# Narrow tiles of a mixture-of-experts tail: gathers ahead of the stores, half buffers for the results, low parts made ahead of the results

## The chip, the core and the metric

One core of a Trainium2 chip runs the whole program. The metric is the device time of one execution in microseconds (us). The kernel before took 1560.92 us (median of three runs, 1560.53 to 1563.27). TensorE (PE) multiplies, VectorE (DVE) and ScalarE (ACT) move and transform what it leaves in PSUM, GpSimd (POOL) issues the indirect DMAs here, SyncE (SP) the plain ones.

## The reference, cut to what matters

The program is a gated cross-attention layer over 16 batches of 256 tokens, followed by a mixture of experts on the normalised rows:

```
x = x + tanh(g_xattn) * cross_attention(ctx, layernorm(x))     # 8 heads of 128
gates = (layernorm(x) @ Wg + bg) / (1 + 1e-6)                  # 8 experts
w, idx = top_k(gates, 2); w = softmax(w)
h = silu(layernorm(x) @ W1[e] + b1[e])                         # 256 -> 1024
y[e] = h @ W2[e] + b2[e]                                       # 1024 -> 256
x = x + tanh(g_ffn) * sum over the two chosen e of w[e] * y[e]
```

All products are made as three passes over a high and a low part of both sides (`product`, L181 to L183: high times low, low times high, high times high). Only the end of the experts' part is touched by the change.

## The kernel before

The 4096 tokens, each with two experts, make 8192 pairs, which are sorted by expert into lists padded to rows of 128 pairs (71 such rows). A tile is the work on one or two of these rows for one expert. The first 31 tiles (`WIDE`) are wide, two rows each; the last 9 (tiles 31 to 39, `NARROW`) are narrow, one row each, since an expert's list can end in half a wide tile. A wide tile takes four steps n on TensorE, a narrow one two; step 124 (`FIRST_N`) is the first narrow one and step 141 the last.

For each tile: POOL gathers the tile's token rows into `xg` (`gather`); TensorE turns them into `px` (`turn_x`); ScalarE and VectorE split them into `xt_hi` and `xt_lo`. For each step TensorE makes the hidden part `ph` (`hidden`) from `xt` and the split first-layer weights `w1s_hi` and `w1s_lo`. In narrow tiles VectorE copies this part to `flat` (`read_flat`), and TensorE turns it with the identity (`turn_hidden`, L1293; the target is called `ph` or `routing`). ScalarE applies silu (`hs`) and makes `ht_hi`, VectorE makes `ht_lo` (`lo_h`, L1664), and TensorE multiplies with the second-layer weights into `py` (`out`). After a tile's last step VectorE's `finish` adds the bias into `yo` (L1700) and multiplies by the pair's weight (L1706). POOL then stores the rows, adding them to the output in memory (`scatter`, L901). SyncE loads 1 MB of first-layer weights per tile (L716) when the low parts of the tile two before are made.

The order on each engine is the order in which the code is written; nothing schedules it. TensorE's loop over n does `turn_x` (every second narrow step), `hidden(n)`, `turn_hidden(n-1)`, `out(n-2)`. So between two `out` pieces stand a hidden part and a turn. VectorE's loop over n does `read_flat(n)`, on even steps `lo_x` and `take_weights`, on odd steps `finish` of the tile before, then `lo_h(n-1)` and the low part of the weights of step n+2 (`w1_lo_two`, L1654). `finish(t)` waits until TensorE's last `out` of tile t is done, reads the expert's number into a register (L619), and waits until the buffer of `yo` is free.

Each added store waits for the one before it (`s_add`), because two of them may touch the same output row. There are two `yo` buffers of two rows; narrow tiles use only the first row of each. POOL's loop over t issues, in this order, the second store of tile t-2 (wide tiles only), the gathers of tile t+2 (or t+3 for narrow ones), the first store of tile t-1. For `xg` there are two buffers of two rows, of which narrow tiles use all four rows in turn.

Of the kernel before, what the change touches and what calls it, by code (L numbers as in the profile page):

```python
# [9 lines left out]
ALU = mybir.AluOpType  # L10
# [4 lines left out]
B, T, D = 16, 256, 256  # L15
# [23 lines left out]
WIDE = (ROWS - NARROW) // 2  # L39
assert 2 * WIDE + NARROW == ROWS and WIDE % 2  # L40
SUB = 2
TILE = SUB * P
N_TILES = WIDE + NARROW
# [41 lines left out]
def subs(t):  # L85
    return SUB if t < WIDE else 1


def row_of(t):
    return SUB * t if t < WIDE else SUB * WIDE + t - WIDE  # L90
# [6 lines left out]
def blocks_of(t):  # L97
    return PB if t < WIDE else 2 * PB


def step_of(t):
    return PARTS * t if t < WIDE else PARTS * WIDE + (t - WIDE) * (FT // (2 * PB))


N_STEPS = step_of(N_TILES)
TILE_OF = [(t, j) for t in range(N_TILES) for j in range(steps_of(t))]

N_RAW, N_PH, N_HS, N_HT, N_XT, N_XG, N_YO = 2, 3, 2, 3, 2, 2, 2
N_W1S = PARTS
LAG = 2  # L110
LEAD = 2
# [219 lines left out]
def layer(nc, programs, A, sem, alloc, space, early, step, work, lists, ident, iota8, lane, dram,  # L331
# [6 lines left out]
    with ExitStack() as ctx:  # L338
# [102 lines left out]
        with ExitStack() as banks:  # L441
            def bank(name):
                return banks.enter_context(nc.psum_tensor(name, [P, 512], F32))
# [11 lines left out]
        with ExitStack() as banks:  # L455
# [3 lines left out]
            py = [over[last_o], bank("py1")]  # L459
# [53 lines left out]
        N_GN = N_XG * SUB  # L513
# [9 lines left out]
        s_l2, s_pyr, s_w, s_yo, s_add = sem("y_pair"), sem("y_read"), sem("w_ready"), sem("y_out"), sem("added")  # L523
# [30 lines left out]
        def w1_parts(n):  # L554

            if n >= N_STEPS or TILE_OF[n][0] < EARLY and TILE_OF[n][0] != HOME_TILES[0]:
                return []
            t, j = TILE_OF[n]
            k = blocks_of(t) // PB
            return [(t, j * k + i) for i in range(k)]  # L560
# [13 lines left out]
        def xg_of(t, s):  # L574
            n = t - WIDE
            return xg[t % N_XG][s] if n < 0 else xg[t % N_XG][n // N_XG % SUB]

        def s_gathered(t):
            return s_g[t % N_XG] if t < WIDE else s_gn[(t - WIDE) % N_GN]

# [4 lines left out]
        def had_rows(t):  # L585

            n = t - WIDE
            return t - N_XG if n < N_XG else WIDE - N_XG + n % N_XG if n < N_GN else t - N_GN
# [26 lines left out]
        def home_of(t):  # L615
            return int(t >= HOME_TILES[0])
# [156 lines left out]
        def _(pool):  # L773
# [39 lines left out]
            def norm_rows(b):  # L813

                pool.wait_ge(s_mvc, b + 1)
                own.mark(pool.tensor_scalar(ve["c"][:, 0:TT], mv_c[:, 0:TT, 1], EPS, 1.0, ALU.add, ALU.mult))
                pow_rstd("c", rs_c, TT, s_rsc)
                negate(mv_c)
                own.wait()
                pool.wait_ge(s_rsc, b + 1)  # L820
                if b >= 2:
                    pool.wait_ge(s_rowst[b % 2], 16 * (b // 2))
                elif b == 0:
                    pool.wait_ge(s_pad, 16 * N_PAD)
                for t in range(TT):
                    last = norm(rows[b % 2][:, t, 0:D], x2[b % 2][:, t, :], mv_c, rs_c, t)
                last.then_inc(s_xn, 1)
# [16 lines left out]
            def list_tokens(b):  # L844

                pool.wait_ge(s_place, b + 1)
                pool.wait_ge(s_pad, 16 * N_PAD)
                if b >= EARLY_B:
                    pool.wait_ge(s_early_names, 32)
                for k in range(TOP):  # L850
                    for t in range(TT):
                        q = k * TT + t
                        pool.indirect_dma_start(
                            out=dram["lists"].rearrange("l (p o) -> (l p) o", o=1),
                            out_offset=bass.IndirectOffsetOnAxis(ap=place[:, q:q + 1].bitcast(U32), axis=0),
                            in_=ids[:, TT * b + t:TT * b + t + 1], in_offset=None,
                        ).then_inc(s_listed, 16)
# [22 lines left out]
            def gather(t, s):  # L880
                if t >= N_XG:

                    pool.wait_ge(s_px, had_rows(t) + 1)
                    pool.wait_ge(s_w, row_of(had_rows(t) + 1))
                u = row_of(t) + s
                source = dram["xhat"][0:EARLY_B * T, :] if t < EARLY else dram["xhat"]
                pool.indirect_dma_start(
                    out=xg_of(t, s)[:, :], out_offset=None, in_=source,
                    in_offset=bass.IndirectOffsetOnAxis(ap=token[:, u:u + 1].bitcast(U32), axis=0),
                ).then_inc(s_gathered(t), 16)  # L890

            def scatter(t, s):
                u = row_of(t) + s
                pool.wait_ge(s_yo, u + 1)
                if u:

                    pool.wait_ge(s_add, 16 * u)
                else:
                    for i in range(2):
                        pool.wait_ge(s_x2st[i], 16 * (B // 2))  # L900
                pool.indirect_dma_start(  # L901
                    out=A["out"], out_offset=bass.IndirectOffsetOnAxis(ap=token[:, u:u + 1].bitcast(U32), axis=0),
                    in_=yo[t % N_YO][:, s, :], in_offset=None, compute_op=ALU.add,
                ).then_inc(s_add, 16)

            for c in range(2):
# [28 lines left out]
                gather(2, s)  # L935
            norm_rows(B - 1)
            for t in range(1, N_TILES + 1):
                if t >= 2 and subs(t - 2) == 2:
                    scatter(t - 2, 1)
                if t + N_XG == EARLY:  # L940
                    pool.wait_ge(s_rowst[1], 16 * (B // 2))
                    pool.wait_ge(s_token, 1)
                for later in (t + N_XG, t + N_XG + 1):
                    if later < N_TILES and (later < WIDE + N_XG) == (later == t + N_XG):
                        for s in range(subs(later)):
                            gather(later, s)
                if t == 2:
                    pool.wait_ge(s_row, 1)
                    pool.wait_ge(s_listed, 16 * TOP * TT * B)
                    pool.indirect_dma_start(  # L950
                        out=names[0:LATE_SUB, 0:P], out_offset=None, in_=dram["lists"],
                        in_offset=bass.IndirectOffsetOnAxis(ap=row[0:LATE_SUB, :].bitcast(U32), axis=0),
                    ).then_inc(s_names, 16)
                scatter(t - 1, 0)
                if t == 1:
                    list_tokens(B - 1)
# [444 lines left out]
        def _(dve):  # L1401
# [249 lines left out]
            def w1_lo_two(t, part):  # L1651
                dve.wait_ge(s_w1hi, w1_before(t) + part + 2)
                hi, lo = (two_parts(s, part) for s in w1s)
                dve.tensor_tensor(lo, raw_parts(t, part), hi.bitcast(F32), ALU.subtract).then_inc(s_w1lo, 2)  # L1654
# [30 lines left out]
            def finish(t):  # L1685

                dve.wait_ge(s_l2, step_of(t + 1))
                if t < EARLY:
                    if t == 0:
                        dve.wait_ge(s_home_b2, 32)  # L1690
                    bias = home_b2[:, home_of(t), :]
                else:
                    e = expert_of(dve, t)
                    if t == EARLY:
                        dve.wait_ge(s_b2, 16)
                    bias = b2[:, bass.ds(e * D, D)]
                if t >= N_YO:
                    dve.wait_ge(s_add, 16 * row_of(t - N_YO + 1))
                n = subs(t)
                dve.tensor_tensor(yo[t % N_YO][:, 0:n, :], py[t % 2][:, 0:n * D].rearrange("p (s d) -> p s d", s=n),  # L1700
                                  bias.unsqueeze(1).to_broadcast([P, n, D]), ALU.add).then_inc(s_pyr, 1)
                dve.wait_ge(s_pyr, t + 1)
                for s in range(n):
                    u = row_of(t) + s
                    dve.wait_ge(s_w, u + 1)
                    dve.tensor_scalar(yo[t % N_YO][:, s, :], yo[t % N_YO][:, s, :], wcol[:, u:u + 1], None, ALU.mult)\  # L1706
                        .then_inc(s_yo, 1)

            def first_spread(half, scale, add):
# [106 lines left out]
            for n in range(2, FIRST_N):  # L1816
                t, j = TILE_OF[n]
# [26 lines left out]
            for n in range(FIRST_N, N_STEPS + 1):  # L1844
                if n < N_STEPS:
                    t, j = TILE_OF[n]
                    read_flat(n)
                    if j == 0 and t + 1 < N_TILES:
                        lo_x(t + 1)
                        take_weights(t + 1)  # L1850
                    if j == 1:
                        finish(t - 1)
                if n > FIRST_N:
                    lo_h(n - 1)
                for t, part in w1_parts(n + LEAD)[::2]:
                    w1_lo_two(t, part)
            finish(N_TILES - 1)


# [21 lines left out]
```

## Time and profile before

| | |
|---|---|
| median of three runs | 1560.92 us |
| the profiled execution's own time | 1558.27 us |
| its span, from the first to the last instruction | 1556.6 us |
| mean granted TensorE clock | 0.99 |
| narrow tiles: from the first narrow px to the last py | 1470.1 to 1546.8 us |

Times in the rows below are microseconds from the start of the span. A timeline row gives the start, the duration, engine, line, operation, what it writes and reads, and in brackets how long its engine sat idle before it and what ended this. The durations of matmuls overlap (they are pipelined), so an engine's pace is read from one start to the next. A row of busy time by stretch gives the stretch and its length, then busy us with the number of instructions for PE, PEld (weight loads), DVE, ACT and POOL, then the granted clock (1.00 is 2.4 GHz), the share of time in which DMA engines were busy, and GB/s.

### The profile page before, as it was taken

The page shows a single profiled execution, that of the slowest core. Times are in us where ns is not written, and L with a number is a line of the kernel's source. Part 1 is how long each engine was busy: PE and PEld are TensorE (multiplying, and loading weights), DVE is VectorE, ACT ScalarE, POOL GpSimd, SP SyncE. Part 2 cuts the span into 40 slices and gives each one's busy share as a digit, 9 for nine tenths or more (in the row PEclk, how much of TensorE's full clock was granted, in tenths as well). Part 3 has the DMA queues.
Part 4 walks back from the last instruction along what each step waited for, and adds up shares of the span by engine and source line. Part 5 has one row for each costly group of instructions (what it writes and reads, how often), then busy time and mean ns, then how long its engine had stood idle before and what let it go on. Part 6 is the DMA issues. An engine that isn't in the chain of part 4 may idle for free. (4 is left out here: it accounts for less than half of the span.)

```text
span 1556.6 us, 29904 instructions
## 1 busy us (share of the span) xinstructions
PE 1503.6 (97%) x10410; PEld 1386.2 (89%) x10410; DVE 1110.2 (71%) x2687; ACT 950.6 (61%) x2060; POOL 604.3 (39%) x714
## 2 busy tenths in 40 slices
PE   6999998999999999999999999999989999999986
PEld 5889887888989889898888988888989999999986
DVE  6777776777777777777777777777786666666674
ACT  5655654565565555555565565555777777777764
POOL 5322423233342433433234342332454544444452
PEclk9999999999999999999999999999999999999998
DMA  4000100001000000000000000022754544554553
GB/s 147 19 21 8 21 8 21 8 22 28 8 22 8 22 28 8 22 8 21 12 17 29 7 22 8 8 75 70 193 128 127 154 131 127 146 139 127 147 157 69
DMA packets 57823, 91.13 MB, mean 59 GB/s; under 512 B 8521, under 2 KB 44774, under 8 KB 57550
## 3 DMA queue, kind: packets, MB, share of 16 engines
q1 hardware_dynamic: 41710, 70.19, 14.0%
q0 software_dynamic: 15824, 18.98, 6.9%
q8 instruction: 88, 1.44, 0.4%
q14 instruction: 57, 0.47, 0.1%
q10 hardware_dynamic: 144, 0.05, 0.0%
HBM read 70.91 MB, written 18.29 MB: 57 GB/s over the span
## 5 line engine op out<-in xcount | busy, mean ns | idle before, releaser
L876 POOL TENSOR_SCALAR probs<-probs,rsum 128x512 f32<-128x512 f32 x256 | 174.1, 692 | 531.6 <-DVE rsum L1547 523.7
L1087 ACT ACTIVATE pt_hi<-turn 128x512 fp32r<-128x512 f32 x256 | 139.3, 595 | 239.7 <-PE turn L1233 239.7
L901 POOL DMA_INDIRECT out_rows<-yo,token x71 | 121.5, 1711 | 213.5 <-DMA out_rows<-yo,token 137.6
L1664 DVE TENSOR_TENSOR ht_lo<-hs,ht_hi 128x512 fp32r<-128x512 f32 x142 | 98.0, 690 | 114.5 <-ACT ht_hi L1052 113.0
L1541 DVE TENSOR_REDUCE smax<-score 128x1 f32<-128x512 f32 x256 | 169.8, 685 | 12.8 <-PE score L183 12.4
L986 ACT ACTIVATE probs<-score,nbias 128x512 f32<-128x512 f32 x256 | 173.0, 685 | 4.2 <-DVE nbias L1543 4.1
L1043 ACT ACTIVATE hs<-ph,vecs 128x256 f32<-128x256 f32 (+1 forms) x284 | 114.2, 457 | 95.6 <-PE ph L183 82.4
L1772 DVE TENSOR_TENSOR pt_lo<-turn,pt_hi 128x512 fp32r<-128x512 f32 x256 | 164.2, 682 | 9.4 <-ACT pt_hi L1087 9.3
L181 PE MATMUL py<-w_hi,ht_lo 128*128 (+1 forms) x568 | 163.9, 289 | 5.8 <-DVE ht_lo L1664 5.8
L182 PE MATMUL py<-w_lo,ht_hi 128*128 (+1 forms) x568 | 161.8, 285 | 0.0
L183 PE MATMUL py<-w_hi,ht_hi 128*128 (+1 forms) x568 | 161.7, 285 | 0.0
L181 PE MATMUL ring<-pt_hi,v_lo 128*128 128x256 f32 x512 | 146.9, 287 | 10.7 <-DVE kt_lo L1444 9.0
L974 ACT ACTIVATE kt_hi<-ring,vecs 128x512 fp32r<-128x512 f32 x128 | 88.3, 690 | 94.5 <-PE ring L183 94.5
L181 PE MATMUL ph<-xt_hi,w1s_lo 128*128 128x256 f32 x496 | 141.4, 285 | 4.7 <-DVE xt_lo L1642 4.6
L183 PE MATMUL ring<-pt_hi,v_hi 128*128 128x256 f32 x512 | 145.5, 284 | 0.0
L182 PE MATMUL ring<-pt_lo,v_hi 128*128 128x256 f32 x512 | 145.3, 284 | 0.0
L183 PE MATMUL ph<-xt_hi,w1s_hi 128*128 128x256 f32 x496 | 139.0, 280 | 0.0
L182 PE MATMUL ph<-xt_lo,w1s_hi 128*128 128x256 f32 x496 | 138.8, 280 | 0.0
L1444 DVE SCALAR_TENSOR_TENSOR qt_lo<-ring,vecs,qt_hi 128x256 fp32r<-128x256 f32 x128 | 61.9, 484 | 106.9 <-ACT qt_hi L976 105.4
L1233 PEld LDWEIGHTS turn<-ident,probs 128*128 128x128 f32 x1024 | 121.4, 142 | 17.4 <-POOL probs L876 0.3
L1233 PE MATMUL turn<-ident,probs 128*128 128x128 f32 x1024 | 134.3, 275 | 0.0
L1444 DVE SCALAR_TENSOR_TENSOR kt_lo<-ring,vecs,kt_hi 128x512 fp32r<-128x512 f32 x128 | 95.9, 749 | 50.7 <-ACT kt_hi L974 42.9
(247 smaller groups left out, 4709.7 us busy)
## 6 DMA issues: line engine op xcount, KB each, us to landing
w_raw<-in_L_ffn_W SPq DMA_DIRECT2D x45, 1024.0 KB, 12.8
xhat_rows<-rows SPq DMA_DIRECT2D x16, 264.0 KB, 2.2
x_raw<-in_x SPq DMA_DIRECT2D x16, 256.0 KB, 3.1
c_raw<-in_ctx SPq DMA_DIRECT2D x16, 256.0 KB, 3.2
out_rows<-x SPq DMA_DIRECT2D x16, 256.0 KB, 2.3
xg<-xhat_rows,token POOLq DMA_INDIRECT x71, 4.3
out_rows<-yo,token POOLq DMA_INDIRECT x71
v_raw<-in_L_xattn_Wkv SPq DMA_DIRECT2D x2, 512.0 KB, 8.6
```

The source lines that it names most:

```text
L181: pe.matmul(out, ll, rh, start=start, stop=False, **kw)
L182: pe.matmul(out, lh, rl, start=False, stop=False, **kw)
L183: return pe.matmul(out, lh, rh, start=False, stop=stop, **kw)
L876: last = pool.tensor_scalar(probs[n % 2][:, t, :], probs[n % 2][:, t, :], rsum[:, n % 2, t:t + 1], 1.0, ALU.mult, ALU.mult)
L901: pool.indirect_dma_start(out=A["out"], out_offset=bass.IndirectOffsetOnAxis(ap=token[:, u:u + 1].bitcast(U32), axis=0), in_=yo[t % N_YO][ ...
L986: act.activation(probs[n % 2][:, t, :], score[t][:, :], ACT.Exp, scale=SCALE, bias=nbias[:, n % 2, t:t + 1], accum_out=ssum[:, n % 2, t:t ...
L1043: last = act.activation(by_step(hs[n % N_HS], t)[:, g, :], by_step(ph[n % N_PH] if t < WIDE else turned_of(n), t)[:, g, :], ACT.Silu, bias ...
L1087: act.activation(pt[0][:, 2 * t:2 * t + 2, :], turn[t][:, :].rearrange("p (j i) -> p j i", j=2), ACT.Copy).then_inc(s_pthi, 1)
L1233: last = pe.transpose(turn[t][:, j * T + q * P:j * T + (q + 1) * P], probs[n % 2][:, q, (2 * t + j) * P:(2 * t + j + 1) * P], ident[:, :])
L1444: dve.scalar_tensor_tensor(out=lo[:, :], in0=part, scalar=bias, in1=hi[:, :].bitcast(F32), op0=ALU.add, op1=ALU.subtract).then_inc(s_read, 1)
L1541: own.mark(dve.tensor_reduce(smax[:, n % 2, t:t + 1], score[t][:, :], AX_X, ALU.max))
L1772: dve.tensor_tensor(pt[1][:, 2 * t:2 * t + 2, :], turn[t][:, :].rearrange("p (j i) -> p j i", j=2), pt[0][:, 2 * t:2 * t + 2, :].bitcast(F ...
```

## The change

Four things change, all in the narrow tiles or just before them.

- POOL's loop issues the gather of narrow tile t+4 (was t+3) for tiles 33 to 39, and does so first in its turn, ahead of the stores. Tiles up to 32 are gathered as before.
- `yo_of` gives narrow tiles one row of a `yo` buffer each, so that four results have room instead of two. The waits follow: a narrow tile's `finish` waits for the store of the tile four before it, where it waited for the one two before it.
- VectorE's narrow loop calls `finish` last in an odd step, behind `lo_h` and `w1_lo_two`.
- `t` is renamed to `later` in one loop, so that `finish(t - 1)` behind it means the same tile.

```
@@ yo_of
+        def yo_of(t):
+            n = (t - WIDE) // N_YO % SUB
+            return yo[t % N_YO][:, :, :] if t < WIDE else yo[t % N_YO][:, n:n + 1, :]
@@ scatter
-                    in_=yo[t % N_YO][:, s, :], in_offset=None, compute_op=ALU.add,
+                    in_=yo_of(t)[:, s, :], in_offset=None, compute_op=ALU.add,
@@ POOL's loop
             for t in range(1, N_TILES + 1):
+                if WIDE + N_XG <= t + N_GN < N_TILES:
+                    gather(t + N_GN, 0)
                 if t >= 2 and subs(t - 2) == 2:
                     scatter(t - 2, 1)
...
-                for later in (t + N_XG, t + N_XG + 1):
-                    if later < N_TILES and (later < WIDE + N_XG) == (later == t + N_XG):
-                        for s in range(subs(later)):
-                            gather(later, s)
+                if t + N_XG < min(N_TILES, WIDE + N_XG):
+                    for s in range(subs(t + N_XG)):
+                        gather(t + N_XG, s)
@@ finish
-                if t >= N_YO:
+                if t >= WIDE + N_YO:
+                    dve.wait_ge(s_add, 16 * row_of(t - SUB * N_YO + 1))
+                elif t >= WIDE:
+                    dve.wait_ge(s_add, 16 * (row_of(t - N_YO) + 1))
+                elif t >= N_YO:
                     dve.wait_ge(s_add, 16 * row_of(t - N_YO + 1))
@@ VectorE's narrow loop
-                    if j == 1:
-                        finish(t - 1)
                 if n > FIRST_N:
                     lo_h(n - 1)
-                for t, part in w1_parts(n + LEAD)[::2]:
-                    w1_lo_two(t, part)
+                for later, part in w1_parts(n + LEAD)[::2]:
+                    w1_lo_two(later, part)
+                if n < N_STEPS and j == 1:
+                    finish(t - 1)
```

The instructions and their number stay the same on every engine, and so does the order on TensorE, ScalarE and SyncE. POOL at the change from wide to narrow tiles, before, from the gather of tile 32 on (`xg1_1` is the second row of buffer 1 and so on; L887 gathers, L901 stores):

```order
L887 DMA xg0_0<-xhat_rows,token 128x264
L887 DMA xg1_1<-xhat_rows,token 128x264
L901 DMA out_rows<-yo1,token 4224x256 x2
L887 DMA xg0_1<-xhat_rows,token 128x264
L901 DMA out_rows<-yo0,token 4224x256 x2
L887 DMA xg1_0<-xhat_rows,token 128x264
L901 DMA out_rows<-yo1,token 4224x256
L887 DMA xg0_0<-xhat_rows,token 128x264
L901 DMA out_rows<-yo0,token 4224x256
L887 DMA xg1_1<-xhat_rows,token 128x264
```

And with the change, from the gather of tile 34 on:

```order
L892 DMA xg0_1<-xhat_rows,token 128x264
L906 DMA out_rows<-yo0,token 4224x256
L892 DMA xg0_0<-xhat_rows,token 128x264
L906 DMA out_rows<-yo1,token 4224x256
L892 DMA xg1_0<-xhat_rows,token 128x264
L906 DMA out_rows<-yo1,token 4224x256
L906 DMA out_rows<-yo0,token 4224x256
L892 DMA xg0_0<-xhat_rows,token 128x264
L906 DMA out_rows<-yo0,token 4224x256
L906 DMA out_rows<-yo1,token 4224x256
L892 DMA xg1_1<-xhat_rows,token 128x264
L906 DMA out_rows<-yo0,token 4224x256
```

The gathers of tiles 34 and 35 now stand ahead of the stores of tiles 28 and 29, those of tiles 36 and 37 ahead of the last store of tile 30 and that of tile 32; each stands one to three stores earlier than it did.

VectorE in the steady part, one odd step and what surrounds it, before (`ISA` and `TENSOR_LOAD` read the expert's number):

```order
L1670 COPY flat1<-ph2 128x512
L619 TENSOR_LOAD expert
L619 ISA x2
L1700 ISA
L1700 TENSOR_TENSOR yo0<-py0,b2 128x256
L1706 TENSOR_SCALAR yo0<-yo0,wcol 128x256
L1664 TENSOR_TENSOR ht1_lo<-hs0,ht1_hi 128x512
L1654 TENSOR_TENSOR w1s_lo<-w1_raw1,w1s_hi 128x2x2x256
L1670 COPY flat0<-ph1 128x512
```

And with the change:

```order
L1676 COPY flat1<-ph2 128x512
L1670 TENSOR_TENSOR ht1_lo<-hs0,ht1_hi 128x512
L1660 TENSOR_TENSOR w1s_lo<-w1_raw1,w1s_hi 128x2x2x256
L624 TENSOR_LOAD expert
L624 ISA x2
L1710 ISA
L1710 TENSOR_TENSOR yo0<-py0,b2 128x256
L1716 TENSOR_SCALAR yo0<-yo0,wcol 128x256
L1676 COPY flat0<-ph1 128x512
```

The result (`yo`, with the register read ahead of it) moved behind the low part `ht_lo` of the hidden values and behind that of the weights, and stands now ahead of the next `flat` copy only.

## Rows read from the trace of the kernel before

**Rows 1.** Busy time by stretch, each from one px to the next; columns explained above.
```profile
1476.52:1484.85 8.33, 7.13 (x60) 6.70 (x58) 6.46 (x12) 6.21 (x15) 5.39 (x3) 1.00 0.49 118
...
1494.74:1503.36 8.62, 8.54 (x58) 8.34 (x58) 5.79 (x11) 4.43 (x12) 5.02 (x4) 0.80 0.59 150
...
1525.15:1532.42 7.27, 7.01 (x60) 6.78 (x59) 6.02 (x11) 5.71 (x14) 1.57 (x1) 1.00 0.50 119
```

**Rows 2.** Timeline of TensorE, narrow tiles: start, duration, idle before and its releaser.
```profile
1479.55 0.38 PE L181 MATMUL py<-w_hi,ht_lo 128*128 x1 [0.83 <-DVE ht_lo L1664]
...
1484.85 0.44 PE L1257 MATMUL px<-ident,xg 128*128 128x128 f32 x2 [0.37 <-DMA xg<-xhat_rows,token]
...
1494.74 0.63 PE L1257 MATMUL px<-ident,xg 128*128 128x128 f32 x2 [2.92 <-DMA xg<-xhat_rows,token]
...
1526.79 0.60 PE L1293 MATMUL ph<-ident,flat 128*128 128x128 f32 x4
1527.65 0.38 PE L181 MATMUL py<-w_hi,ht_lo 128*128 x1 [0.26 <-DVE ht_lo L1664]
...
1530.55 0.60 PE L1293 MATMUL routing<-ident,flat 128*128 128x128 f32 x4
1530.91 0.36 PE L181 MATMUL py<-w_hi,ht_lo 128*128 x1
...
1534.93 0.38 PE L181 MATMUL py<-w_hi,ht_lo 128*128 x1 [0.53 <-DVE ht_lo L1664]
...
1542.20 0.38 PE L181 MATMUL py<-w_hi,ht_lo 128*128 x1 [1.90 <-DVE ht_lo L1664]
...
1546.55 0.28 PE L183 MATMUL py<-w_hi,ht_hi 128*128 x1
```

**Rows 3.** Timeline of POOL: gathers (L887) and added stores (L901).
```profile
1478.02 1.58 POOL L901 DMA_INDIRECT out_rows<-yo,token  x1 [5.68 <-DMA out_rows<-yo,token]
...
1482.53 2.27 POOL L901 DMA_INDIRECT out_rows<-yo,token  x1 [1.09 <-DMA out_rows<-yo,token]
1489.46 1.79 POOL L901 DMA_INDIRECT out_rows<-yo,token  x1 [4.66 <-DVE wjunk L1681]
1491.55 1.02 POOL L887 DMA_INDIRECT xg<-xhat_rows,token  x1 [0.30 <-issue]
...
1521.27 1.57 POOL L901 DMA_INDIRECT out_rows<-yo,token  x1 [3.37 <-DMA out_rows<-yo,token]
1528.66 1.57 POOL L901 DMA_INDIRECT out_rows<-yo,token  x1 [5.81 <-DMA out_rows<-yo,token]
...
1541.74 1.75 POOL L901 DMA_INDIRECT out_rows<-yo,token  x1 [5.52 <-DVE yo L1706]
1548.70 1.55 POOL L901 DMA_INDIRECT out_rows<-yo,token  x1 [5.21 <-DVE yo L1706]
```

**Rows 4.** Timeline of VectorE around the results and low parts.
```profile
1481.53 0.69 DVE L1664 TENSOR_TENSOR ht_lo<-hs,ht_hi 128x512 fp32r<-128x512 f32 x1
...
1494.38 0.42 DVE L1700 TENSOR_TENSOR yo<-py,b 128x256 f32<-128x256 f32 x1 [2.43 <-DMA out_rows<-yo,token]
...
1526.09 0.43 DVE L1700 TENSOR_TENSOR yo<-py,b 128x256 f32<-128x256 f32 x1 [1.20 <-PE py L183]
...
1526.82 0.68 DVE L1664 TENSOR_TENSOR ht_lo<-hs,ht_hi 128x512 fp32r<-128x512 f32 x1
1527.42 1.22 DVE L1654 TENSOR_TENSOR w1s_lo<-w_raw,w1s_hi 128x1024 fp32r<-128x1024 f32 x1
1528.56 0.68 DVE L1670 COPY flat<-ph 128x512 f32<-128x512 f32 x1
```

**Rows 5.** Timeline of ScalarE: the high part that the low part of rows 4 follows.
```profile
1525.20 0.63 ACT L1052 ACTIVATE ht_hi<-hs 128x512 fp32r<-128x512 f32 x1
```

**Rows 6.** Timeline of SyncE's queue: the last load of first-layer weights.
```profile
1522.53 0.01 SPq L716 DMA_DIRECT2D w_raw<-in_L_ffn_W  x1
```

**Rows 7.** DMA traffic, 1520 to 1530 us, in 40 slices of 0.25 us.
```profile
GB/s 393 17 0 0 0 0 0 0 0 0 0 0 98 115 33 33 147 344 393 475 344 475 426 393 442 393 221 201 246 37 0 0 0 33 0 0 0 0 0 0
```

More of the change, by code:

```diff
@@ L1696, in finish @@
                     bias = b2[:, bass.ds(e * D, D)]
-                if t >= N_YO:
+                if t >= WIDE + N_YO:
[3 more added lines that the diff above has]
+                elif t >= N_YO:
                     dve.wait_ge(s_add, 16 * row_of(t - N_YO + 1))
                 n = subs(t)
-                dve.tensor_tensor(yo[t % N_YO][:, 0:n, :], py[t % 2][:, 0:n * D].rearrange("p (s d) -> p s d", s=n),
+                dve.tensor_tensor(yo_of(t), py[t % 2][:, 0:n * D].rearrange("p (s d) -> p s d", s=n),
                                   bias.unsqueeze(1).to_broadcast([P, n, D]), ALU.add).then_inc(s_pyr, 1)
@@ L1705, in finish @@
                     dve.wait_ge(s_w, u + 1)
-                    dve.tensor_scalar(yo[t % N_YO][:, s, :], yo[t % N_YO][:, s, :], wcol[:, u:u + 1], None, ALU.mult)\
+                    dve.tensor_scalar(yo_of(t)[:, s, :], yo_of(t)[:, s, :], wcol[:, u:u + 1], None, ALU.mult)\
                         .then_inc(s_yo, 1)
```

## The prediction

> **What bounds the kernel now.** I read the page's slices first: TensorE is busy nine tenths nearly everywhere, and only the last slices fall off. So I went to the narrow tiles with three views in turn: the busy time of each engine from one px to the next, TensorE's timeline with its idle times, and the timelines of POOL and VectorE for what stood in front.
>
> The reader is to see four things. First, a steady narrow tile lasts 7.27 us with TensorE busy for 7.01 of it [rows 1]. Inside it one matmul waits: the turn of the hidden part starts at 1526.79 and the `py` that follows starts 0.86 later, while the same pair four us on, which waits for nothing, stands 0.36 apart (1530.55, 1530.91) [rows 2]. So 0.50 us is lost per tile, although the row prints 0.26 idle: a matmul's modelled end lies after the next one's possible start. TensorE's own pace is 7.27 - 0.50 = 6.77 us a tile. Second, gathers come late: for tile 34 (0.37 idle at 1484.85) and for tile 35 (2.92 at 1494.74). After the second the clock is at 0.80 on the average of the next stretch, thus partly at 1.2 GHz, and the stretch takes 8.62 us [rows 1, 2]. Third, gather 35 was issued at 1491.55, behind a store that could not start until 1489.46 [rows 3]. The stores are a chain, each waiting for the one before. Fourth, `ht_lo` at 1526.82 starts 0.99 after its input `ht_hi` was ready (1525.20 + 0.63); in between VectorE waits for TensorE's last `py` of a tile, reads a register and makes the result [rows 4, 5]. This is what the matmul at 1527.65 waits for. The same happens at 1479.55 (0.83), 1534.93 (0.53) and 1542.20 (1.90) [rows 2].
>
> **The gathers.** The order puts gather 34 ahead of the second store of tile 28, gather 35 ahead of that of tile 29 and gather 36 ahead of that of tile 30. Each needs a buffer whose tile has been turned by then, so none waits. A gather costs POOL 1.0 to 1.9 us of issue, and it is put where POOL sits idle for the store chain anyway (4.66 to 5.68 us ahead of the stores of rows 3); gather 35 would be issued about 1472.6 and gather 36 about 1485, the latter to be turned only at 1497. A gather's data is queued behind a store or a weight load at times; even 7.4 us to landing, the longest that rows 3 show for a store, leaves 2.5 us or more of room. I cost the move at nothing and take both gather waits and the slow clock away. If a gather did land late, the row at 1494.74 says what it costs.
>
> **The half buffers** add no instruction. Today `finish` of tile 32 waits 2.43 us until 1494.38 for a store [rows 4], hidden now only because TensorE is waiting for gather 35 until 1494.74. With gathers alone this would be late next, as `flat` and `ht_lo` stand behind it. With room for four, tile t needs the store of tile t-4. The walk of the store chain below has that store done 5 us or more ahead each time, so this wait goes.
>
> **The low parts first.** In the steady tile `ht_lo` can start at 1525.87 instead of 1526.82, 0.95 earlier, and its `py` follows 0.83 after (1526.82 to 1527.65): 1526.70, before the 1527.15 at which TensorE is ready. The 0.50 us a tile goes. What moves back is the result: VectorE makes the weights' low part right behind `ht_lo` (until about 1527.6), then the result, at the latest about 1528.4 if the register read of some 0.7 is not hidden, and then `flat` at about 1529.1 instead of 1528.56 [rows 4]. TensorE turns this `flat` at 1530.55 [rows 2], or 0.5 earlier without its own wait, and 1529.1 + 0.69 is before that. VectorE is busy 6.02 and ScalarE 5.71 us a tile [rows 1], both under 6.77. The bounds of this edit: it gives 0.50 a tile, or, if the store chain or `flat` takes over, down to nothing.
>
> **TensorE's sum.** From the px at 1476.52 to the start of step 140 at 1532.42 lie seven tiles and 55.90 us; at 6.77 they are 47.39. That frees 8.51 us, all the stalls named and the slow clock among them. One is not freed: around the first narrow tiles the two-row result of tile 30 now stands ahead of the `ht_lo` that starts at 1481.53 [rows 4], with the same work in front of it as before. TensorE would be there at 1481.79 and gets it at about 1482.5, so I charge 0.77 (between 0.6 and 1.07, the stall that was there before): 7.74. The wait at 1534.93 comes 1.12 after the turn where 0.36 would do: 0.76 more, 8.50. At the end `ht_lo` again stands behind a result: 0.95 more, 9.45. Then the last matmul, at 1546.55 now, starts at 1537.1, and the last store could be issued 2.15 later as now (1546.55 to 1548.70 [rows 2, 3]): 1539.25. If the shorter last wait also keeps the clock up, this is 1538.15 (the last 24 matmuls take 4.35 us now and would take 2.86 at their steady 0.119; of the 1.49 I count 1.1, as the second half then waits a little for its own `ht_lo`).
>
> **The stores' sum.** They may be later than TensorE. A store that meets no weight load lets the next one start 4.51 us after it (1478.02 to 1482.53). One that is issued just before a load's data takes 7.39 (1521.27 to 1528.66) [rows 3]: the load was issued at 1522.53 [rows 6], traffic runs at 350 to 475 GB/s from 1524.2 to 1526.4 and only then falls to the store's level [rows 7], and the next store starts 6.13 after the load's issue. With the change a weight load is issued every 6.77 us, so a store that follows a caught one starts 6.13 after one load's issue and 0.64 ahead of the next. The store of 1521.27 started 1.26 ahead of its load's issue and was caught, so this one is too: one store per load. The second store of tile 30 starts at about 1488 to 1489.5 and is caught; the stores of tiles 31 to 34 follow one per load. The last load comes now at 1522.53, 4.67 after the px of tile 38 (1517.86 by the sum of tiles). That px moves to 1511.1, and the load's low parts no longer stand behind the result, about 1.0 less: it is issued at 1514.8. The store of tile 35 then starts at 1514.8 + 6.13 = 1520.9, at most 1521.3. Four more at 4.51: 1539.3 for the last. So the two sums end within 0.1 us of each other, and the stores are the later by a hair.
>
> **Sum.** The last store starts at 1539.3 instead of 1548.70, and the 7.9 us behind it stay: 9.4 us less. The profiled execution (1558.27 us) becomes 1548.9. The median of the runs is 2.65 above the profiled one, so from 1560.92 I predict 1551.5.
>
> The Trainium skill's "DMA: Bandwidth & Descriptors", section "Queues, rings and completion order", says that each DMA engine takes turns between its queues packet by packet. By that rule a store would share with a load and not stand behind it, and its pace would stay near 4.5 us. Rows 3 and 7 speak against it in this kernel (7.39 us, with the load's traffic first). What it would make of the time is the third rival.
>
> **Rivals.**
>
> 1. The store chain keeps today's pace. Six stores from 1489.46 take 39.2 us to 1528.66 [rows 3], mean 6.53; three more at 4.51 give 1542.2, a gain of 6.5: 1554.4 us. For it: in the same stretch loads will come closer together, not less often. Against it: today's late ones are locked to a load period of 7.27, which shrinks.
> 2. TensorE's pace stays 7.27, since the chain from turn over silu, high and low part to `py` is itself too long, or `flat` comes late. Then 4 x 0.50, 0.76 and half of the end stay, and with the loads later the stores follow: a gain of about 5.5, 1555.4 us. Against it: 0.95 is freed where 0.50 is needed.
> 3. Stores are not caught by loads. Then TensorE's end decides, with the clock up: the last store at 1538.15, a gain of 10.5: 1550.4 us.
> 4. The gathers land late all the same (a load's data ahead of them): the 2.92 idle and the slow clock, together some 4.9 us, stay: a gain of 4.5, 1556.4 us, and in the mildest form within the noise.
> 5. Slower. One mechanism: results now follow the issue of the weight load instead of preceding it, so every store sits behind 1 MB. From 1489.46 nine stores reach the last one, today at a mean of 6.58 us. Over 6.93 the kernel is measurably slower. At the longest interval seen, 7.39, the last starts at 1556.0: 7.3 us more, 1568.2 us. Against it: the last five stores meet no load.
>
> **How the numbers follow.** Forecast 0.50, rivals in order 0.17, 0.13, 0.11, 0.06, 0.03. The forecast's own range is 1550 to 1553 (a store more or less in the cleared part, and the runs' own spread). Taking in rivals 1 to 3 the range is 1549.5 to 1556.8. A measurement of this kernel tells no change from one of 0.2%, 3.1 us. All of the forecast and of rivals 1 to 3 but 0.01, and most of rival 4, are faster by more: 0.93. Within 0.2%: 0.04. Slower: 0.03.
>
> **What would show it.** In the profile after: no px waits for a gather; the stretch after tile 35's px has clock 1.00; steady px stand 6.8 apart; `py` follows the turn by 0.36; `yo` starts behind the weights' low part; intervals of the stores are near 6.8 until the last weight load and 4.5 after it; the last store starts near 1539. I am wrong if px stay 7.27 apart, if the last stores wait for `yo` instead of one another (rival 3), or if the stores' mean interval from the last wide one on stays above 6.

## The result

The changed kernel took 1551.95 us, median of six runs (1550.09 to 1552.95), against 1560.64 us of the kernel before on the same chips (six runs, 1557.59 to 1563.27). The ratio of their times is 0.9948, with a 95% interval of 0.9938 to 0.9959: 0.5% faster, 8.7 us in the medians. 1551.5 was predicted. The profiled execution took 1550.09 us with a span of 1548.4 us, 8.2 us less than in the kernel before.

The last store starts at 1540.64 instead of 1548.70 [rows 3]; what follows it is as long as before (7.8 us; 7.9 then). From the px of tile 33 (1476.41; 1476.52 before) to it are 64.23 us instead of 72.18. This length is the best measure of what the narrow tiles take, since what stands before them varies (see the last section).

Busy time of the changed kernel by stretch, each from one px to the next, tiles 33 to 38, answering to [rows 1]:

```profile
1476.41:1484.19 7.78, 7.27 (x60) 6.80 (x59) 6.68 (x13) 6.67 (x16) 2.98 (x2) 1.00 0.59 149
1484.19:1491.13 6.94, 6.93 (x59) 6.76 (x59) 5.88 (x11) 4.95 (x13) 4.17 (x3) 1.00 0.71 217
1491.13:1498.46 7.33, 7.16 (x58) 6.76 (x59) 6.46 (x12) 6.14 (x14) 2.90 (x2) 1.00 0.51 142
1498.46:1505.35 6.89, 6.89 (x59) 6.78 (x59) 5.98 (x11) 5.26 (x14) 2.77 (x2) 1.00 0.59 183
1505.35:1512.78 7.43, 7.20 (x60) 6.79 (x59) 6.54 (x12) 6.28 (x15) 2.59 (x2) 1.00 0.56 184
1512.78:1519.62 6.84, 6.84 (x59) 6.76 (x59) 5.97 (x11) 5.16 (x14) 1.57 (x1) 1.00 0.64 195
```

The clock is 1.00 in each: the slow stretch is gone. Behind tile 33 (7.78 us, 8.33 before) the tiles last 6.84 to 6.94 and 7.33 to 7.43 us in turn, instead of 7.27 (and 9.89 and 8.62 for tiles 34 and 35). TensorE's timeline, answering to [rows 2]:

```profile
1496.01 0.60 PE L1299 MATMUL routing<-ident,flat 128*128 128x128 f32 x4
1496.78 0.38 PE L181 MATMUL py<-w_hi,ht_lo 128*128 x1 [0.17 <-DVE ht_lo L1670]
...
1498.46 0.41 PE L1263 MATMUL px<-ident,xg 128*128 128x128 f32 x2
...
1535.21 0.38 PE L181 MATMUL py<-w_hi,ht_lo 128*128 x1 [0.96 <-DVE ht_lo L1670]
...
1537.09 0.38 PE L181 MATMUL py<-w_hi,ht_lo 128*128 x1 [0.18 <-DVE ht_lo L1670]
...
1538.49 0.28 PE L183 MATMUL py<-w_hi,ht_hi 128*128 x1
```

No px waits for a gather. But at 1496.78 `py` stands 0.77 behind the turn, where 0.36 is the pace; at 1511.08 it is 0.82. That is every second tile. The wait at the end has shrunk from 1.90 to 0.96.

POOL, answering to [rows 3] (L892 gathers, L906 stores):

```profile
1472.70 0.99 POOL L892 DMA_INDIRECT xg<-xhat_rows,token  x1 [0.30 <-issue]
...
1485.20 1.89 POOL L892 DMA_INDIRECT xg<-xhat_rows,token  x1 [0.30 <-issue]
1487.85 1.57 POOL L906 DMA_INDIRECT out_rows<-yo,token  x1 [0.75 <-DMA out_rows<-yo,token]
1493.48 1.89 POOL L906 DMA_INDIRECT out_rows<-yo,token  x1 [4.06 <-DMA out_rows<-yo,token]
...
1501.22 1.57 POOL L906 DMA_INDIRECT out_rows<-yo,token  x1 [4.54 <-DMA out_rows<-yo,token]
...
1508.09 1.58 POOL L906 DMA_INDIRECT out_rows<-yo,token  x1 [3.79 <-DMA out_rows<-yo,token]
...
1515.53 1.57 POOL L906 DMA_INDIRECT out_rows<-yo,token  x1 [4.54 <-DMA out_rows<-yo,token]
1522.30 1.65 POOL L906 DMA_INDIRECT out_rows<-yo,token  x1 [5.21 <-DMA out_rows<-yo,token]
1526.99 1.55 POOL L906 DMA_INDIRECT out_rows<-yo,token  x1 [3.04 <-DMA out_rows<-yo,token]
1531.54 1.70 POOL L906 DMA_INDIRECT out_rows<-yo,token  x1 [3.00 <-DMA out_rows<-yo,token]
1536.22 1.55 POOL L906 DMA_INDIRECT out_rows<-yo,token  x1 [2.98 <-DVE yo L1716]
1540.64 1.55 POOL L906 DMA_INDIRECT out_rows<-yo,token  x1 [2.87 <-DVE yo L1716]
```

Gathers 35 and 36 are issued at 1472.70 and 1485.20; gather 35 was at 1491.55. The stores come 5.6 to 7.7 us apart up to that of tile 35 (1522.30) and then 4.42 to 4.69. SyncE's queue, answering to [rows 6], issues the last weight load here:

```profile
1516.05 0.17 SPq L721 DMA_DIRECT2D w_raw<-in_L_ffn_W  x1
```

VectorE, answering to [rows 4]:

```profile
1491.69 0.69 DVE L1670 TENSOR_TENSOR ht_lo<-hs,ht_hi 128x512 fp32r<-128x512 f32 x1 [0.42 <-ACT ht_hi L1058]
1492.71 1.23 DVE L1660 TENSOR_TENSOR w1s_lo<-w_raw,w1s_hi 128x1024 fp32r<-128x1024 f32 x1 [0.33 <-ACT w1s_hi L1038]
1493.85 0.42 DVE L1710 TENSOR_TENSOR yo<-py,b 128x256 f32<-128x256 f32 x1
1494.30 0.67 DVE L1716 TENSOR_SCALAR yo<-yo,wcol 128x256 f32<-128x256 f32 x1
1494.89 0.67 DVE L1676 COPY flat<-ph 128x512 f32<-128x512 f32 x1
...
1495.95 0.68 DVE L1670 TENSOR_TENSOR ht_lo<-hs,ht_hi 128x512 fp32r<-128x512 f32 x1
...
1501.22 0.35 DVE L1716 TENSOR_SCALAR yo<-yo,wcol 128x256 f32<-128x256 f32 x1
...
1540.01 0.35 DVE L1716 TENSOR_SCALAR yo<-yo,wcol 128x256 f32<-128x256 f32 x1
```

ScalarE's `ht_hi`, the input of the two `ht_lo` above:

```profile
1491.03 0.63 ACT L1058 ACTIVATE ht_hi<-hs 128x512 fp32r<-128x512 f32 x1
...
1494.68 0.63 ACT L1058 ACTIVATE ht_hi<-hs 128x512 fp32r<-128x512 f32 x1
```

The `ht_lo` that had to wait for a result before now starts 0.03 us after `ht_hi` is ready (1491.69 after 1491.66). The result comes behind the weights' low part, and `flat` and the next `ht_lo` behind that: this one starts at 1495.95, 0.64 after its `ht_hi` (1495.31), and 0.83 later starts the `py` that waited. The last result ends at 1540.36 and its store starts 0.28 later, 4.42 after the one before it. So results and stores reach the end together, as the two sums had it.

### The profile page after: what moved, and what is told of

Same layout as the page of the kernel before. It is cut to its first block and busy times, and to the rows that moved or that the text cites. A ratio compares the mean times of both kernels' runs of the same rounds, so it can differ in the third digit from the quotient of the medians.

```text
span 1548.4 us, 29904 instructions
## 1 busy us (share of the span) xinstructions
PE 1501.3 (97%) x10410; PEld 1383.4 (89%) x10410; DVE 1112.3 (72%) x2687; ACT 954.0 (62%) x2060; POOL 603.0 (39%) x714
## 5 line engine op out<-in xcount | busy, mean ns | idle before, releaser
L906 POOL DMA_INDIRECT out_rows<-yo,token x71 | 120.6, 1699 | 206.4 <-DMA out_rows<-yo,token 149.2
```

What stands on the lines that cost most here:

```text
L906: pool.indirect_dma_start(out=A["out"], out_offset=bass.IndirectOffsetOnAxis(ap=token[:, u:u + 1].bitcast(U32), axis=0), in_=yo_of(t)[:, s ...
```

## The experiments

Twelve experiments: eleven further kernels, and the changed one again, each run 6 to 12 times. Ratios are to the kernel before on the same chip, with 95% intervals. The narrow part is the time from the px of tile 33 to the start of the last store in the one profiled execution of each kernel; the changed kernel's two profiled executions differ in it by 0.43 us.

| kernel | ratio | narrow part, us |
|---|---|---|
| before | 1 | 72.18 |
| changed | 0.9948 (0.9938 to 0.9959) | 64.23 |
| gathers alone | 0.9973 (0.9959 to 0.9986) | 68.92 |
| low parts first alone | 0.9972 (0.9956 to 0.9987) | 69.96 |
| all but low parts first | 0.9955 (0.9936 to 0.9973) | 66.56 |
| all but half buffers | 0.9946 (0.9926 to 0.9966) | 64.54 |
| changed, again | 0.9949 (0.9930 to 0.9968) | 63.80 |
| gathers three ahead | 1.0006 (0.9989 to 1.0022) | 75.46 |
| four ahead, not first | 0.9960 (0.9945 to 0.9976) | 68.03 |
| finish in between | 0.9959 (0.9943 to 0.9975) | 63.73 |
| half loads | 0.9937 (0.9919 to 0.9955) | 63.20 |
| in between, half loads | 0.9928 (0.9910 to 0.9947) | 63.48 |
| split loads | 0.9949 (0.9929 to 0.9968) | 63.65 |
| split loads, in between | 0.9939 (0.9921 to 0.9956) | 64.12 |

**The change taken apart.** First the new gathers alone, with the buffers and the place of `finish` as before:

```
+                if WIDE + N_XG <= t + N_GN < N_TILES:
+                    gather(t + N_GN, 0)
                 if t >= 2 and subs(t - 2) == 2:
                     scatter(t - 2, 1)
```

> Gathers early alone: the two result buffers and the place of finish stay as before. My theory: the two gather waits and the slow clock go (0.53 + 3.1 + 1.6, some 5 us), the 0.50 us per steady tile and the 1.9 us wait at the end stay, and now and then finish waits for a store, about 0.5 us in all. Last store near 1544.0 instead of 1548.70; 0.3% faster than before. Rival (the order on VectorE matters little): the whole 0.52% of the change is here. Rival (two buffers stop it): finish of tile 32 waits to 1494.4 as before and most of the gain is lost, under 0.1%.

The ratio agrees. The narrow part gains 3.3 us, 1.4 less than the 4.7 I gave it. I let `finish` wait some 0.5 us for stores in all; that of tile 32 alone waits 3.21 us, and the `py` behind it, at 1499.20, prints 2.29 us of idle time. This is the wait that the second rival named; it took a part of the gain and not most of it.

```profile
1497.64 0.42 DVE L1701 TENSOR_TENSOR yo<-py,b 128x256 f32<-128x256 f32 x1 [3.21 <-DMA out_rows<-yo,token]
```

The move of `finish` alone:

```
-                    if j == 1:
-                        finish(t - 1)
                 if n > FIRST_N:
                     lo_h(n - 1)
...
+                if n < N_STEPS and j == 1:
+                    finish(t - 1)
```

> finish behind the low parts alone: gathers and result buffers as before. My theory: gather 35 is still issued behind the store chain near 1491.5, so px of tile 35 stays near 1494.7 with its idle and the slow clock; from there each tile gains 0.2 to 0.5 us, the wait at 1534.93 goes (0.76) and half of the last one (0.95). Last store near 1546.0, 0.15% faster. Rival (stores decide the end): the chain of stores stays where it was until the loads end and the gain is under 1 us.

The profile agrees with my theory (2.2 us of the narrow part where I gave it 2.7; the px of tile 35 still waits 2.25 us, that of tile 34 another 2.06). The ratio is better than that, 0.28%, and the profiled execution was the second slowest of its twelve (1560.4 with a median of 1554.8), so what the others did is not seen. The rival (under 1 us) fell by both.

Then the change without each of its other parts: with `finish` put back to its place (the lines above in reverse), and with two whole buffers (`yo_of` and its waits taken out).

> Gathers early and half buffers, finish in its old place ahead of the low parts. My theory: like gathers alone, but no wait of finish for a store; px 7.27 apart throughout; last store near 1543.5, 0.33% faster than before. Against the kernel with two buffers (gathers alone) the difference is 0.5 us or less. Rival (half buffers carry a good part): 1.5 us or more faster than gathers alone.

> The whole change but the half buffers: finish of tile t waits for the store of tile t-2. In the changed kernel stores 31 to 34 are done about when results 33 to 36 are made (store 32 by 1507.8, result 34 at 1508.1), so my theory is waits of 0 to 0.5 us at three or four results, each passed on by half to TensorE: last store near 1541.5, 0.45% faster than before, within 1 us of the changed kernel. Rival (the buffers are needed): each result waits for a store that is locked to the weight loads, TensorE falls to the stores' pace, and over 2.5 us of the gain go.

With the result first, half buffers give 2.4 us (68.92 to 66.56): here the rival was right, and the wait of 3.21 us shown above is gone. With the low parts first they give 0.3 to 0.7 (64.54 to 64.23 and 63.80), within the noise of the ratios: my theory held, no `finish` waits for a store there, and the rival fell. The place of `finish` gives 2.3 to 2.8 with half buffers and 4.4 without. So the parts overlap: late gathers, a result that waits for a store ahead of `ht_lo`, and a result that waits for `py` ahead of `ht_lo` hold up the same engine, and each edit uncovers the next. Gathers and low parts first alone already make 7.6 of the 8.0 to 8.4 us. These lengths come from one execution each; of the steps between the kernels with early gathers, only those over 1 us are clear of the 0.43 us above, and their ratios do not tell them apart.

**The changed kernel again**, beside the three that follow:

> The changed kernel again, on the chip and against the runs of the three kernels beside it: 0.5% faster than before, last store near 1540.6, px alternately 6.9 and 7.35 apart.

The ratio and the narrow part came as expected (last store 1542.59 after a px of tile 33 that is 2.38 us later). The tiles take 6.75 to 6.95 and 7.14 to 7.20 us in turn, so every second one is shorter than I expected by some 0.2 us. Here the multiplication of the result by the pair's weight takes 0.35 to 0.37 us each time, never 0.67, and `py` stands 0.63 and 0.53 us behind the turn (1498.76, 1512.74).

**How far ahead must the gather be?** Three tiles ahead as before but first in POOL's turn (`t + N_XG + 1` for `t + N_GN`):

> The changed kernel with narrow gathers three tiles ahead as before, but still first in POOL's turn, ahead of the stores. Theory: the place ahead of the stores does most of it: gather 35 is issued near 1485 instead of 1491.5 and has landed by 1490, just before px of tile 35 at 1491.1; gathers 36 to 39 land 1 to 6 us ahead or up to 1 us late where a load is in front. Same as the changed kernel within 1 us. Rival (the fourth tile is needed): px of tiles 35 to 39 wait 1 to 3 us for gathers and half of the gain goes.

My theory fell, and the rival did not go far enough: the whole gain is gone, with eleven of the twelve runs between 1558.2 and 1567.6. TensorE and POOL of this kernel:

```profile
1497.03 0.44 PE L1263 MATMUL px<-ident,xg 128*128 128x128 f32 x2 [2.17 <-DMA xg<-xhat_rows,token]
...
1511.78 0.69 PE L1263 MATMUL px<-ident,xg 128*128 128x128 f32 x2 [7.81 <-DMA xg<-xhat_rows,token]
```

```profile
1482.55 2.02 POOL L906 DMA_INDIRECT out_rows<-yo,token  x1 [5.01 <-issue]
1490.85 1.55 POOL L906 DMA_INDIRECT out_rows<-yo,token  x1 [6.28 <-DVE yo L1716]
1492.70 1.04 POOL L892 DMA_INDIRECT xg<-xhat_rows,token  x1 [0.30 <-issue]
1497.41 1.69 POOL L906 DMA_INDIRECT out_rows<-yo,token  x1 [3.67 <-DMA out_rows<-yo,token]
1504.96 1.68 POOL L906 DMA_INDIRECT out_rows<-yo,token  x1 [5.86 <-DMA out_rows<-yo,token]
1506.95 1.02 POOL L892 DMA_INDIRECT xg<-xhat_rows,token  x1 [0.30 <-issue]
```

Gather 36 can only be issued behind the store of tile 31 (1504.96), at 1506.95, and the px waits 7.81 us. In this execution the chain of stores runs one load later than in the changed kernel: the store at 1482.55 takes 8.30 us to the next, where 4.65 were enough in the changed one (1478.14 to 1482.79). In SyncE's queue the next weight load was issued 1.31 us behind the store at 1482.55 (1483.86) and 2.00 behind that at 1478.14 (1480.14). The row at 1490.85 names `yo`, but tile 30's result was made by 1484.5, so this wait too was for the store before. A gather that stands behind the chain inherits this; one that stands a store or two earlier does not. One thing stays open: the kernel with the low parts first alone has its narrow gathers no earlier in the order than this one, and yet gained 0.28%, with an interval just clear of this one's. So the distance alone does not say why all of the gain went. The opposite case, four ahead but behind the gathers of wide tiles and a wide tile's second store:

```
-                if WIDE + N_XG <= t + N_GN < N_TILES:
-                    gather(t + N_GN, 0)
                 if t >= 2 and subs(t - 2) == 2:
                     scatter(t - 2, 1)
                 if t + N_XG < min(N_TILES, WIDE + N_XG):
...
+                if WIDE + N_XG <= t + N_GN < N_TILES:
+                    gather(t + N_GN, 0)
```

> The changed kernel with the gather of tile t+4 at the end of POOL's gathers, behind the second store of a wide tile and ahead of the first store: four tiles ahead, but not first. For narrow tiles the place is the same, so only gathers 34 and 35 and that of 36 move behind one store. Theory after the three-ahead run (gathers of tiles 35 and 36 2.2 and 7.8 us late): the fourth tile is what matters, since the chain of stores runs up to three stores behind; this kernel is within 0.5 us of the changed one, no px waits for a gather. Rival (the place ahead of the stores matters): gather 36 is issued behind the second store of tile 30, near 1490 instead of 1485, and still lands by 1496, so even then at most 0.5 us.

Its twelve runs lie between 1549.7 and 1560.9, and the profiled one is the slowest of them. In it one px waits 2.31 us, and the store of the same place (1485.48) takes 8.61 us to the next, the one before it 8.02. My theory, no wait and 0.5 us at most, fell for this execution; over all runs the ratio (0.9960) cannot be told from that of the changed kernel (0.9949). So the fourth tile decides whether there is a gain. That being first protects it against a late chain is not shown: it rests on one execution of each of the two kernels.

**What holds the stores?** Half of the first-layer weights are left out of the last six loads (the kernel then multiplies by stale weights in half of those columns):

```
+                cols = slice(0, F if t < WIDE + 3 else F // 2)
```

> The changed kernel with half of the first-layer weights left out of the last six loads (tiles 34 to 39; the other half of the buffer is stale). If a store is held up by the load in front of it, intervals of the stores of tiles 30 to 34 fall from 6.8 to 7.4 to about 5 us, the chain catches up with the results by about tile 34, and each store then waits for its result. The end: results and stores tie in the changed kernel, so the last store comes 0 to 0.5 us earlier. If DMA engines took turns fairly between store and load, intervals would shrink by half a load at most in proportion to shared traffic and the chain would not catch up before the last load. If the intervals do not change, they are not due to the loads.

POOL's stores in it, from the first store of tile 30 on:

```profile
1485.48 2.58 POOL L907 DMA_INDIRECT out_rows<-yo,token  x1 [3.56 <-DVE wjunk L1688]
...
1490.88 1.57 POOL L907 DMA_INDIRECT out_rows<-yo,token  x1 [0.62 <-issue]
1495.72 1.55 POOL L907 DMA_INDIRECT out_rows<-yo,token  x1 [3.27 <-DMA out_rows<-yo,token]
...
1500.19 1.84 POOL L907 DMA_INDIRECT out_rows<-yo,token  x1 [1.54 <-DMA out_rows<-yo,token]
...
1504.99 1.57 POOL L907 DMA_INDIRECT out_rows<-yo,token  x1 [1.64 <-DVE yo L1717]
...
1512.01 1.57 POOL L907 DMA_INDIRECT out_rows<-yo,token  x1 [3.37 <-DVE yo L1717]
```

The intervals are 5.40, 4.84, 4.47 and 4.80, and then 7.02: from there each store waits for its result. So the loads made the long intervals, as my theory had it. The last store comes only 0.6 to 1.0 us earlier by the narrow part (63.20 against 63.80 and 64.23): the results, which tied with the stores before, now hold it.

**Can VectorE's wait be filled?** It waits 0.33 us for the weights' high part ahead of the low part in every step with a result (1492.71). `finish` between the two:

```
                 if n > FIRST_N:
                     lo_h(n - 1)
+                if n < N_STEPS and j == 1:
+                    finish(t - 1)
                 for later, part in w1_parts(n + LEAD)[::2]:
                     w1_lo_two(later, part)
```

> The changed kernel with finish between lo_h and w1_lo_two. In the changed one VectorE stands idle 0.33 us ahead of the weights' low part (it waits for ScalarE's high part) in each step, and finish behind it makes flat and the next ht_lo late, which costs TensorE 0.45 us in every other tile. Theory: finish fills the idle 0.33, the wait of TensorE goes, px stand 6.8 to 6.9 apart; the stores follow the loads, which come closer too; last store near 1539.3, 1.0 to 1.5 us faster than the changed kernel. Rival (stores decide): px close up but the last store moves under 0.4 us. Rival (finish ahead of the weights' low part delays hidden): no change or slower.

The px close up to 6.79 to 7.15 (from 6.84 to 7.43) and no `py` waits in the steady part, but the narrow part is as long: the rival, that the stores decide. Result and stores at its end (VectorE, then POOL):

```profile
1538.61 0.35 DVE L1716 TENSOR_SCALAR yo<-yo,wcol 128x256 f32<-128x256 f32 x1
```

```profile
1535.62 1.55 POOL L906 DMA_INDIRECT out_rows<-yo,token  x1 [2.96 <-DMA out_rows<-yo,token]
1540.08 1.55 POOL L906 DMA_INDIRECT out_rows<-yo,token  x1 [2.92 <-DMA out_rows<-yo,token]
```

The last result is ready at 1538.96 and its store starts 1.12 later, behind the chain. With the loads halved as well, and then with whole loads issued in two halves, the first as soon as its half of the buffer is free, without and with `finish` in between:

```
+                    for half in range(2):
+                        sp.wait_ge(s_w1lo, w1_before(t - N_RAW) + (half + 1) * PARTS // 2)
+                        load_w1_half(t, half)
```

> finish between lo_h and w1_lo_two, and half of the first-layer weights left out of the last six loads. Theory: with finish in between, the end is set by the stores' chain alone (result 39 was made by 1538.96, its store started only at 1540.08, waiting for the one before). With the loads halved the chain catches up and the last store follows its result: from the px of tile 33 to the last store 62.5 us (63.7 with whole loads, 63.8 to 64.2 in the changed kernel). Rival (the loads have no part in it): 63.7 again.

> The changed kernel with the last six weight loads in two halves, the first half issued as soon as the low parts of the first half of the tile two before are made, some 3.3 us earlier. Same bytes. Theory: a store stands behind 0.5 MB at most, its interval falls from 6.8 to 7.4 to about 5 to 6.3 us, under TensorE's pace, and the chain catches up by tile 35; the end in the changed kernel is a tie of results and stores, so the last store comes 0 to 0.5 us earlier. Rival: stores are now caught twice, 7 us or more each, no change or up to 3 us slower.

> Split loads and finish between lo_h and w1_lo_two together, the whole computation. Theory: neither stores nor results hold the other up: 62.5 us from the px of tile 33 to the last store, 1.2 to 1.7 us less than the changed kernel, 0.6% faster than before. Rival (stores caught twice): as with finish in between alone, 63.7.

None reached 62.5 us. With `finish` as in the change, split loads gave the tie (63.65). With `finish` in between and half loads, the stores of tiles 31 to 35 stayed 6.6 to 7.0 us apart (63.48), so both theories of 62.5 us fell. POOL in the last one:

```profile
1497.47 2.15 POOL L921 DMA_INDIRECT out_rows<-yo,token  x1 [4.66 <-DMA out_rows<-yo,token]
...
1504.36 2.26 POOL L921 DMA_INDIRECT out_rows<-yo,token  x1 [3.42 <-DMA out_rows<-yo,token]
...
1511.35 2.20 POOL L921 DMA_INDIRECT out_rows<-yo,token  x1 [3.41 <-DMA out_rows<-yo,token]
...
1518.28 2.28 POOL L921 DMA_INDIRECT out_rows<-yo,token  x1 [3.40 <-DMA out_rows<-yo,token]
...
1541.39 1.55 POOL L921 DMA_INDIRECT out_rows<-yo,token  x1 [2.93 <-DMA out_rows<-yo,token]
```

The intervals are 6.89, 6.99 and 6.93, the pace of TensorE. Their issue takes 2.15 to 2.28 us here, where 1.57 was usual. That this and the half load in front together keep the chain at the length of a tile is argued and not shown, and why the issue is longer I did not settle. The ratio of this last kernel, 0.9939, is the best of those that compute everything, but its interval holds the changed kernel's 0.9948: no better version is shown.

## Why the prediction was right

**Gathers.** Right: issued at 1472.70 and 1485.20, as worked out to 0.2 us, no px waits, the clock stays up. That the place ahead of the stores costs nothing was right too: behind gather 36 POOL still waits 0.75 us for the store chain. What I had not seen is how much the fourth tile was needed.

**Low parts first.** The mechanism was right, `ht_lo` starts 0.03 after its input. The mis-sized term is TensorE's pace, 6.77 us a tile. From the px of tile 34 to that of tile 39 are 35.43 us, 7.09 a tile, 0.32 more. I let the weights' low part follow `ht_lo` at once; it waits 0.33 for ScalarE, the result and `flat` come that much later, and in every second tile of this execution the multiplication takes 0.67 instead of 0.35. Then `ht_lo` of the next even step starts 0.64 after its input, and its `py` comes 0.41 late. In the changed kernel's second profile, where the multiplication takes 0.35, `py` is still 0.17 to 0.27 late, so each of the two has its part. That the wait for ScalarE matters is borne out by `finish` in between, where no steady `py` waits. The first narrow tile cost 1.01 over the pace where 0.77 was charged. The last matmul started at 1538.49, not 1537.1 or 1536.0.

**Stores.** The mechanism was right. The second store of tile 30 and those of tiles 31 to 35 start at 1487.85, 1493.48, 1501.22, 1508.09, 1515.53 and 1522.30, one per load, and those of tiles 31 to 35 each 6.15 to 6.45 us after the issue of the load before them, where 6.13 was charged. The store of tile 35 was predicted at 1520.9 to 1521.3. It is 1.0 to 1.4 late because the loads follow TensorE's pace: the last was issued at 1516.05, not 1514.8. The four intervals after it were 4.69, 4.55, 4.68 and 4.42 against 4.51. So the last store came at 1540.64 instead of 1539.3, a gain of 8.1 in the profiled execution instead of 9.4. The medians differ by 8.7. That 1551.5 came within 0.5 us of the measured 1551.95 is in part luck: six runs of the kernel before spread over 5.7 us, and the term above was 1.3 us off.

**Half buffers.** As predicted, the wait for a buffer is next in line with gathers alone (3.21 us in `finish`, 2.4 us of the narrow part). With the low parts first the half buffers hardly matter, which I had not said.

**Rivals.** The first, the chain at today's pace, was nearer than I gave it credit for. The six intervals behind the second store of tile 30 take 39.14 us (1487.85 to 1526.99), and today's six took 39.20. The chain started 1.61 earlier, and more of its stores were caught by loads that came closer together. The last store, at 1540.64, lies about halfway between my 1539.3 and this rival's 1542.2. The second, TensorE's pace staying at 7.27, was true of every second tile. It cost 1.3 us and not 3.9, as the others ran at 6.84 to 6.94. The third, stores not caught by loads, is wrong in its cause: half loads shortened the intervals. But its sign came for the last two stores, whose rows name `yo`, each starting 0.28 after its result. Up to that of tile 37 they wait for one another. So the end is a tie, as the two sums had it. The fourth, late gathers, did not come. Nor did the slower case: the nine intervals behind the second store of tile 30 have a mean of 5.87, under the 6.58 of before and the 6 named as a sign.

## What to carry to other kernels

Where several engines wait in front of one another, an edit's worth depends on which others are in: take the change apart in pairs, not singly. Place a prefetch that an engine issues in order with a chain of dependent stores ahead of that chain by as much as the chain can run late, not by as much as it runs late in one profile. When two chains end together, speeding up one alone gives little: `finish` in between made the results earlier and half loads the stores, and neither took more than 1.0 us off the narrow part.

## What the runs showed of the hardware

- A TENSOR_SCALAR of 128x256 f32 in SBUF takes 0.35 us (1501.22, where POOL's issue starts at the same moment) but 0.67 at 1494.30, 0.82 after POOL began the issue of a store. In the changed kernel all three of 0.66 to 0.67 fall 0.5 to 0.8 us into such an issue. In the kernel with split loads and `finish` in between the slow ones (0.47 to 0.52) fall about 0.6 to 0.8 us into a gather's issue. In the narrow tiles of all fourteen profiles the nineteen that begin 0.5 to 1.1 us into an issue take 0.45 to 0.68, the twelve that begin in its first 0.44 us take 0.35, and so do four that begin 1.36 to 1.38 us into one. That one slows the other is argued from this: no run took the issue away alone. The Trainium skill's "VectorE: DVE Perf Modes", section "Two Vector instructions with no wait between them", says in passing that VectorE's second SBUF read interface is shared with GpSimd; this agrees, and does not prove it.
- In the changed kernel, an idle time of 0.96 us at the end left TensorE's clock at 1.00 (1534 to 1540 us); in the kernel before, one of 1.90 was followed by a mean clock of 0.75 in 1542 to 1550.
- What stands before the px of tile 33 is the same work in all kernels, with the place of the first narrow gathers as its main difference, and yet this px starts between 1473.75 and 1483.38 in the profiles. Late gathers of the first wide tiles are one cause. In the latest one (four ahead, not first) a px waits 3.06 us where the changed kernel's (1167.40) does not wait, and from the px before these to the one behind them it takes 4.0 us longer. The px that waits:

```profile
1170.52 1.12 PE L1263 MATMUL px<-ident,xg 128*128 128x128 f32 x4 [3.06 <-DMA xg<-xhat_rows,token]
```

- Runs of one kernel spread over 3 to 14 us, so a difference of 1 us between two kernels is seen in their narrow parts, if at all, and not in their ratios.
